# Four sends in a row on GpSimd: the order of low parts and scatter DMAs in a mixture-of-experts loop

## The chip, the cores and the metric

The kernel runs on one core of one Trainium2 chip. The metric is the device time of one execution in microseconds (us). The engines are named as in the profile: PE (TensorE), DVE (VectorE), ACT (ScalarE), POOL (GpSimd) and SP (SyncE, which only starts DMAs here).

## The reference

A block of four layers over x of shape (32, 16, 16, 64), in float32: windowed attention, an involution (per-pixel 3x3 kernels), a channel attention with a first mixture of experts, and a linear attention with a second mixture. Each layer's output is added to its input. The change lies in the last mixture, `_L3_ffn_ref`, of 8192 tokens with 64 channels, 8 experts and a hidden width of 682:

```python
logits = flat @ router_w.T
probs = jax.nn.softmax(logits, axis=-1)
topk_probs, topk_idx = jax.lax.top_k(probs, TOP_K)          # two experts a token
h = jax.nn.silu(h1) * h3                                    # h1, h3: the token through w1, w3
y = jnp.einsum('neh,ech->nec', h, w2)
out = jnp.einsum('ne,nec->nc', gates, y)
```

## The kernel before

The stages follow each other; the experts of the last mixture are one of the last. Before it, POOL has scattered each token's row, as two float16 halves (high and low), to a list in HBM (`slots`), sorted by expert, twice a token (`send5`, L708). The lists are cut into 39 tiles of 512 rows (`NT` = 39), each of one expert; empty tiles and ends hold dump rows. Tile t does this:

- SP loads the tile's 512 rows into one of two buffers XS (`load5`, L549 to 555), once the buffer's last tile is turned and its ids are copied.
- PE turns it (`turn5`, L2151), ACT copies it as XT (L1632).
- The hidden width is cut into six blocks k of 114 (`NHB`, `HB`). For each, PE makes the two up products in four float16 matmuls (L2189), ACT takes the silu of one (L1655), DVE multiplies it by the other into H5 (L1350, counted as `hid5`). ACT rounds H5 to float16, the high part HI5 (`high5`, L1638). The low part LO5 = H5 - HI5 is made by DVE for k = 0, 1, 3, 4 (`low5`, L1360) and by **POOL for k = 2 and 5** (`low5_pool`, L738 to 743). PE's eight down matmuls of the block (`down5`, L2162 to 2172) wait for the low part.
- After block 5, ACT and DVE sum the tile's result into one of two buffers Y5 (L1646 and L1366, counted as `y5`).
- POOL scatters Y5 to `results` in HBM by four indirect DMAs of 128 rows (`results5`, L727 to 733), with row numbers from IDS, which it copies from the loaded tile (`ids5`, L721 to 725).

Every engine takes its instructions in the program's order, and semaphores count what is done. The orders that matter here:

- H5, HI5, LO5 and the up banks are three deep, by k % 3. So DVE's product for block k waits for the low part of block k - 3 (L1349), that for k = 5 for low 2.
- PE runs three blocks behind with the down matmuls (L2184 to 2198): up 3, down 0, up 4, down 1, the next tile's turn, up 5, down 2, and then up 0 of the next tile, down 3, up 1, down 4, up 2, down 5, up 3. Down 5 of a tile thus stands between up 2 and up 3 of the next.
- ACT takes the silu of block n first, then the high part of block n - 1 (L1655 to 1657): the high part of block 5 stands behind the silu of the next tile's block 0. The copy of the sum (L1646) follows at k = 2 of the next tile, and waits until the scatter of two tiles before has landed (`resulted`).
- POOL's loop over t (L745 to 755) has low 2 of tile t, two sends of tile t - 1, low 5 of tile t, the other two sends of tile t - 1, and the copy of the ids of tile t + 1. Pass 0 has no sends, pass 39 sends only.

After the last send, SP waits for all landings (L565), loads the results back in token order, ACT and DVE weigh and add them, and SP stores the output.

Of the kernel before, what the change touches and what calls it, by code (L numbers as in the profile page):

```python
# [113 lines left out]
def network(nc, xw_d, xi_d, mats_d, vecs_d, feats_d, cw1_d, wmask_d, taps_d, wexp_d,  # L114
            w1l2_d, w2l2_d, w1l3_d, w3l3_d, w2l3_d, out_d, slots_d, results_d):
    with ExitStack() as ctx:
# [5 lines left out]
        def S(step):  # L122

            name = PLACE.get(step, (step, 0))[0]
            if name not in sems:
                sems[name] = nc.alloc_semaphore(name)
            return sems[name]

        def when(step, n):

            return S(step), PLACE.get(step, (step, 0))[1] + n
# [445 lines left out]
        def _(pool):  # L577
# [143 lines left out]
            def ids5(t):  # L721
                if t >= 4:
                    pool.wait_ge(*when(f"resulted_{t % 2}", 16 * SUB * (t // 2 - 1)))
                pool.wait_ge(*when(f"loaded_xs_{t % 2}", 16 * (t // 2 + 1)))
                nc.gpsimd.tensor_copy(IDS[t % 4], XS[t % 2].bitcast(U32)[:, :, C]).then_inc(S("ids5"), 1)

            def results5(t, subs):  # L727
                pool.wait_ge(*when("y5", t + 1))
                pool.wait_ge(*when("ids5", t + 1))
                for i in subs:  # L730
                    pool.indirect_dma_start(  # L731
                        results_d, bass.IndirectOffsetOnAxis(ap=IDS[t % 4][:, i:i + 1], axis=0),
                        Y5[t % 2][:, i, :], None).then_inc(S(f"resulted_{t % 2}"), 16)
# [4 lines left out]
            def low5_pool(t, k):  # L738
                n = t * NHB + k
                pool.wait_ge(*when("high5", n + 1))  # L740
                if n >= 3:
                    pool.wait_ge(*when("down5", n - 2))
                nc.gpsimd.tensor_tensor(LO5[k % 3], H5[k % 3], HI5[k % 3], ALU.subtract).then_inc(S("low5_pool"), 1)  # L743

            for t in range(NT + 1):  # L745
                if t < NT:
                    low5_pool(t, 2)
                if t >= 1:
                    results5(t - 1, (0, 1))
                if t < NT:  # L750
                    low5_pool(t, 5)
                if t >= 1:
                    results5(t - 1, (2, 3))
                    if t + 1 < NT:
                        ids5(t + 1)

# [1619 lines left out]
```

## Time and profile before

| | |
|---|---|
| median of 3 runs | 1143.75 us (1141.32 to 1145.54) |
| the profiled execution | 1143.18 us, span 1141.0 us |
| mean granted clock of PE, as a share of 2.4 GHz | 0.913 |
| busy: PE, DVE, ACT, POOL | 932.4, 801.0, 696.8, 684.4 us |
| POOL's lows (L743), sends (L731) | 78 of 1156 ns, 156 of 984 ns |
| the experts' first low 2 (784.26 us) to the last send's end | 331 us |

The span is the time from the first to the last instruction of the profiled execution. Busy times of several engines overlap. A row of the timeline has start, duration, engine, line, operation, output and input, the count, and in brackets the engine's idle time before it with what ended it. Rows of PE show a group of matmuls whose end includes their latency, so one group's row can reach into the next; the distance from start to start is the pace. "issue" in brackets is idle time that no recorded instruction ended.

### The profile page before, as it was taken

The page shows a single profiled execution, that of the slowest core. Times are in us where ns is not written, and L with a number is a line of the kernel's source. Part 1 is how long each engine was busy: PE and PEld are TensorE (multiplying, and loading weights), DVE is VectorE, ACT ScalarE, POOL GpSimd, SP SyncE. Part 2 cuts the span into 40 slices and gives each one's busy share as a digit, 9 for nine tenths or more (in the row PEclk, how much of TensorE's full clock was granted, in tenths as well). Part 3 has the DMA queues.
Part 4 walks back from the last instruction along what each step waited for, and adds up shares of the span by engine and source line. Part 5 has one row for each costly group of instructions (what it writes and reads, how often), then busy time and mean ns, then how long its engine had stood idle before and what let it go on. Part 6 is the DMA issues. An engine that isn't in the chain of part 4 may idle for free.

```text
span 1141.0 us, 21776 instructions
## 1 busy us (share of the span) xinstructions
PE 932.4 (82%) x6816; PEld 564.5 (49%) x6816; DVE 801.0 (70%) x1647; ACT 696.8 (61%) x1295; POOL 684.4 (60%) x784
## 2 busy tenths in 40 slices
PE   5969999969997899589788875007999999999970
PEld 3445555534445754244355453005776776766650
DVE  7976667668856545787668886305888888887865
ACT  1845555546453276556676663006888888888875
POOL 2945555533778520477406777772777777777770
PEclk9979999989999699599899997558999999999995
DMA  5000000020004100000200000100111111111106
GB/s 217 1 2 1 1 1 1 2 70 0 1 25 124 51 1 0 1 1 14 70 1 22 25 26 25 64 26 24 32 37 31 37 31 32 37 31 35 32 24 224
DMA packets 25473, 39.37 MB, mean 35 GB/s; under 512 B 6340, under 2 KB 14296, under 8 KB 25112
## 3 DMA queue, kind: packets, MB, share of 16 engines
q1 hardware_dynamic: 16280, 28.62, 7.9%
q0 software_dynamic: 9088, 9.39, 2.7%
q8 instruction: 61, 1.00, 0.4%
q14 instruction: 44, 0.36, 0.1%
HBM read 24.52 MB, written 13.47 MB: 33 GB/s over the span
## 4 chain that ended last, share of the span: by engine, by line
PE 35%; POOL 31%; issue 14%; DVE 10%; ACT 7%; DMA 1%; POOLq 0%; SPq 0%; DVEq 0%; ACTq 0%
POOL results L731 11%; POOL slots L708 10%; POOL stage L743 7%; PE bank L1737 6%; PE bank L1748 3%; PE bank L1739 2%; PE bank L1814 2%; POOL stage L690 2%; PE bank L1762 2%; DVE T L816 1%; ACT T L328 1%; ACT T L326 1%; PE bank L1831 1%; PE bank L1866 1%; PE bank L1765 1%
## 5 line engine op out<-in xcount | busy, mean ns | idle before, releaser
L2189 PE MATMUL bank<-stage,big 128*114 128x512 f16 x936 | 243.8, 383 | 1.2 <-ACT stage L1632 1.0
L1350 DVE TENSOR_TENSOR T<-bank,T 114x512 f32<-114x512 f32 x234 | 161.6, 690 | 116.9 <-ACT T L1655 115.9
L731 POOL DMA_INDIRECT results<-stage,small x156 | 153.5, 984 | 37.7 <-issue 35.4
L708 POOL DMA_INDIRECT slots<-T,index x128 | 126.7, 990 | 79.2 <-DVE index L1261 41.6
L1655 ACT ACTIVATE T<-bank 114x512 f32<-114x512 f32 x234 | 139.8, 598 | 40.6 <-PE bank L2189 40.5
L2169 PEld LDWEIGHTS bank<-l2w,stage 114*128 114x128 f16 x1872 | 120.8, 97 | 56.3 <-issue 17.7
L1638 ACT ACTIVATE stage<-T 114x512 f16<-114x512 f32 x234 | 145.5, 622 | 0.2 <-DVE T L1350 0.2
L2169 PE MATMUL bank<-l2w,stage 114*128 x1872 | 143.4, 219 | 2.2 <-POOL stage L743 1.2
L2189 PEld LDWEIGHTS bank<-stage,big 128*114 x936 | 108.3, 131 | 46.8 <-issue 9.1
L743 POOL TENSOR_TENSOR stage<-T,stage 114x512 f16<-114x512 f32 x78 | 90.2, 1156 | 49.7 <-ACT stage L1638 49.7
L1360 DVE TENSOR_TENSOR stage<-T,stage 114x512 f16<-114x512 f32 x156 | 106.9, 685 | 0.0
L1413 ACT ACTIVATE stage<-stage 128x512 f32<-128x512 f32 x64 | 40.3, 630 | 79.4 <-DVE stage L841 79.4
L837 DVE TENSOR_REDUCE small<-bank 128x8 f32<-128x512 f32 x64 | 44.3, 692 | 55.9 <-PE bank L1739 55.9
L621 POOL TENSOR_TENSOR stage<-T,vecs 128x128 f32<-128x128 f32 x64 | 26.6, 415 | 85.1 <-PE bank L1739 85.1
L1737 PE MATMUL bank<-stage 128*128 128x512 f32 x128 | 72.9, 652 | 0.0
L625 POOL TENSOR_TENSOR stage<-T,small 128x512 f32<-128x512 f32 x64 | 67.5, 1055 | 0.0
L645 POOL TENSOR_TENSOR stage<-stage 128x512 f16<-128x512 f32 x40 | 46.1, 1159 | 34.2 <-ACT stage L1469 33.2
L2158 PE MATMUL bank<-ident,stage 128*128 128x128 f16 x156 | 15.4, 221 | 60.5 <-DMA stage<-slots 60.5
L1632 ACT ACTIVATE stage<-bank 128x512 f16<-128x512 f32 x39 | 23.0, 589 | 62.4 <-PE bank L2158 62.4
L690 POOL TENSOR_TENSOR stage<-stage 128x256 f16<-128x256 f32 x64 | 43.0, 690 | 26.8 <-DVE stage L1125 26.3
L909 DVE TENSOR_TENSOR stage<-bank,big 128x512 f32<-128x512 f32 x72 | 46.9, 688 | 9.3 <-PE bank L1831 7.0
L1996 PE MATMUL bank<-T,mats 128*128 128x512 f32 x64 | 36.8, 667 | 15.0 <-ACT T L1545 15.0
(381 smaller groups left out, 1989.7 us busy)
## 6 DMA issues: line engine op xcount, KB each, us to landing
stage<-slots SPq DMA_DIRECT2D x39, 130.0 KB, 2.1
stage<-in_w1l SPq DMA_DIRECT2D x8, 342.0 KB
stage<-in_w3l SPq DMA_DIRECT2D x8, 342.0 KB
results<-stage,small POOLq DMA_INDIRECT x156, 2.2
T<-in_xw SPq DMA_DIRECT2D x4, 512.0 KB, 5.7
X<-in_xi SPq DMA_DIRECT2D x1, 2048.0 KB, 14.0
slots<-T,index POOLq DMA_INDIRECT x128, 2.2
X<-results SPq DMA_DIRECT2D x8, 256.0 KB, 5.9
```

The source lines that it names most:

```text
L625: nc.gpsimd.tensor_tensor(KX[s].rearrange("p (h k) -> p h k", h=HEADS), T2[:, bass.ds(n * WT, WT)].unsqueeze(1).broadcast_to([P, HEADS, WT ...
L690: nc.gpsimd.tensor_tensor(HID_LO[n % 4], HID[n % 4], HID_HI[n % 4], ALU.subtract).then_inc(S("low3"), 1)
L708: pool.indirect_dma_start(slots_d, bass.IndirectOffsetOnAxis(ap=index[:, k, n:n + 1], axis=0), rows5[:, n * RW:(n + 1) * RW], None).then_i ...
L731: pool.indirect_dma_start(results_d, bass.IndirectOffsetOnAxis(ap=IDS[t % 4][:, i:i + 1], axis=0), Y5[t % 2][:, i, :], None).then_inc(S(f" ...
L743: nc.gpsimd.tensor_tensor(LO5[k % 3], H5[k % 3], HI5[k % 3], ALU.subtract).then_inc(S("low5_pool"), 1)
L1350: nc.vector.tensor_tensor(H5[q], bank[3 + q][0:HB, :], S5[q], ALU.mult).then_inc(S("hid5"), 1)
L1360: nc.vector.tensor_tensor(LO5[q], H5[q], HI5[q], ALU.subtract).then_inc(S("low5"), 1)
L1638: nc.scalar.activation(HI5[q], H5[q], ACT.Copy).then_inc(S("high5"), 1)
L1655: nc.scalar.activation(S5[q], bank[q][0:HB, :], ACT.Silu).then_inc(S("silu5"), 1)
L1737: nc.tensor.matmul(bank[s][:, :], QB[s], KX[s], start=True, stop=False)
L2169: mm = nc.tensor.matmul(bank[6 + s][:, i * 128:(i + 1) * 128], H[:, i * 128:(i + 1) * 128], downs[:, bass.ds(w, 2 * C)], start=(k == 0 and ...
L2189: mm = nc.tensor.matmul(bank[q + 3 * (v // 2)][0:HB, :], big16[:, bass.ds(e * (4 * HID3) + (v * HID3 + k * HB), HB)], XT[s], start=(v % 2 ...
```

## The change

POOL makes low 2 and low 5 of a tile one after the other, and then sends the four parts of the tile before in a row.

```diff
@@ -745,12 +745,10 @@
             for t in range(NT + 1):
                 if t < NT:
                     low5_pool(t, 2)
-                if t >= 1:
-                    results5(t - 1, (0, 1))
                 if t < NT:
                     low5_pool(t, 5)
                 if t >= 1:
-                    results5(t - 1, (2, 3))
+                    results5(t - 1, (0, 1, 2, 3))
                     if t + 1 < NT:
                         ids5(t + 1)
```

## Rows read from the trace of the kernel before

**Rows 1.** Stretches: length; busy us (count) of PE, PEld, DVE, ACT, POOL; clock; DMA; GB/s.

```profile
245.00:246.00 1.00, 0.10 (x2) 0.10 (x4) 0.69 (x1) 0.13 (x1) 0.20 (x1) 0.84 0.83 235
...
690.00:695.00 5.00, 3.25 (x17) 2.79 (x18) 2.93 (x8) 1.95 (x3) 3.78 (x5) 1.00 0.10 28
...
850.00:1000.00 150.00, 149.78 (x1364) 105.08 (x1361) 121.40 (x198) 132.13 (x251) 115.37 (x126) 1.00 0.12 34
```

**Rows 2.** The page's chain that ended last, by line, shares of the span.

```profile
POOL results L731 11%; POOL slots L708 10%; POOL stage L743 7%; PE bank L1737 6%; PE bank L1748 3%; PE bank L1739 2%; PE bank L1814 2%; POOL stage L690 2%; PE bank L1762 2%; DVE T L816 1%; ACT T L328 1%; ACT T L326 1%; PE bank L1831 1%; PE bank L1866 1%; PE bank L1765 1%
```

**Rows 3.** Waits, 792 to 1108 us: us in total, times, longest us.

```profile
POOL stage L743 <- ACT stage L1638: 39.1, 73, 2.9
```

**Rows 4.** Timeline of POOL alone in the experts stage.

```profile
792.49 1.16 POOL L743 TENSOR_TENSOR stage<-T,stage 114x512 f16<-114x512 f32 x1 [2.85 <-ACT stage L1638]
...
867.90 1.15 POOL L743 TENSOR_TENSOR stage<-T,stage 114x512 f16<-114x512 f32 x1 [0.24 <-ACT stage L1638]
869.22 1.00 POOL L731 DMA_INDIRECT results<-stage,small  x1 [0.16 <-issue]
...
872.26 1.15 POOL L743 TENSOR_TENSOR stage<-T,stage 114x512 f16<-114x512 f32 x1 [0.76 <-ACT stage L1638]
873.57 0.99 POOL L731 DMA_INDIRECT results<-stage,small  x1 [0.16 <-issue]
874.87 0.97 POOL L731 DMA_INDIRECT results<-stage,small  x1 [0.30 <-issue]
875.83 0.21 POOL L725 COPY small<-stage 128x4 uint32<-128x4 uint32 x1
876.27 1.16 POOL L743 TENSOR_TENSOR stage<-T,stage 114x512 f16<-114x512 f32 x1 [0.23 <-ACT stage L1638]
...
1102.98 1.15 POOL L743 TENSOR_TENSOR stage<-T,stage 114x512 f16<-114x512 f32 x1 [0.25 <-ACT stage L1638]
...
1106.59 1.17 POOL L743 TENSOR_TENSOR stage<-T,stage 114x512 f16<-114x512 f32 x1
...
1110.49 0.97 POOL L731 DMA_INDIRECT results<-stage,small  x1 [0.30 <-issue]
1111.77 0.97 POOL L731 DMA_INDIRECT results<-stage,small  x1 [0.31 <-issue]
...
1114.32 0.97 POOL L731 DMA_INDIRECT results<-stage,small  x1 [0.30 <-issue]
```

**Rows 5.** Timeline of the other engines in the same cycle.

```profile
869.19 0.60 PEld L2169 LDWEIGHTS bank<-l2w,stage 114*128 114x128 f16 x8
...
869.26 0.68 DVE L1360 TENSOR_TENSOR stage<-T,stage 114x512 f16<-114x512 f32 x1
...
869.96 1.07 PE L2189 MATMUL bank<-stage,big 128*114 128x512 f16 x4
...
871.06 0.60 ACT L1655 ACTIVATE T<-bank 114x512 f32<-114x512 f32 x1 [0.39 <-PE bank L2189]
...
871.55 0.62 ACT L1638 ACTIVATE stage<-T 114x512 f16<-114x512 f32 x1
...
873.55 0.45 PEld L2169 LDWEIGHTS bank<-l2w,stage 114*128 114x128 f16 x8 [0.36 <-issue]
...
874.01 1.03 PE L2189 MATMUL bank<-stage,big 128*114 128x512 f16 x4
...
875.32 1.03 PE L2189 MATMUL bank<-stage,big 128*114 128x512 f16 x4
...
875.57 0.62 ACT L1638 ACTIVATE stage<-T 114x512 f16<-114x512 f32 x1
```

**Rows 6.** Timeline of PE alone, two idle pieces in earlier stages.

```profile
245.91 1.97 PE L1773 MATMUL bank<-T,mats 128*64 128x512 f32 x4 [2.10 <-DVE T L846]
...
691.24 1.99 PE L2046 MATMUL bank<-T,KVS 128*128 128x256 f32 x8 [1.98 <-DVE KVS L1186]
```

**Rows 7.** DMA issues of the page: KB each, us to landing.

```profile
results<-stage,small POOLq DMA_INDIRECT x156, 2.2
```

## The prediction

> **What bounds the kernel now.** I read the stretches first: in the experts stage PE is busy 149.78 of 150 us at clock 1.00, POOL only 115.37 [rows 1]. The page's chain puts "POOL results L731" at its head with 11% [rows 2]. That could mislead: it walks back through POOL's queue, gaps between sends and all. So I turned to what POOL waits for: L743 waits 39.1 us for ACT over 73 instances [rows 3]. The timeline of one tile then shows who is early. Call the low part of block k "low k". POOL starts low 2 at 867.90, sends two sums, idles 0.76 us until ACT's high part comes, starts low 5 at 872.26, sends two more, copies the ids (0.21 us at 875.83), idles 0.23 us, and starts the next low 2 at 876.27 [rows 4]. Both lows start when ACT delivers; the sends fit in the pauses, with 0.76 and 0.23 us to spare. This cycle is 8.37 us long. From the first low 2 with sends behind it (792.49) to the last (1102.98) there are 37 cycles, 310.49 / 37 = 8.39 us each [rows 4].
>
> PE's own work in a cycle is nearly as long. One k step (four up matmuls, eight down) takes 1.31 us, 874.01 to 875.32; the eight down are 0.46 of it, 873.55 to 874.01, so the four matmuls of the turn, as wide, some 0.2: 6 x 1.31 + 0.2 = 8.1 us [rows 5]. Most of what PE loses is the 0.36 us in front of the down matmuls of k = 5: POOL's low ends at 873.41, their weights load at 873.55 [rows 4, 5]. So **PE bounds the stage, with POOL's low parts right beside it**, and what matters is not how many sends POOL has, but how many stand between two lows.
>
> **What the change does.** It adds and removes no instruction: a pass of POOL's loop stays two lows, four sends, one copy. Two of the sends (two DMA issues a pass) move from between low 2 and low 5 to behind low 5. So the first half of a cycle has no send, and the second has four, in 37 passes.
>
> *Half one, low 2 to low 5.* Low 5 starts when ACT hands over, not when POOL is free, so taking two sends from ahead of it gains nothing [rows 4]. That high part stands on ACT behind the silu of the next tile's first block, this on PE behind the down matmuls that wait for low 2. Once low 2 is late the path is: low and hand-over to PE 1.29 us (as 872.26 to 873.55), down matmuls to the next up 0.46, up to silu 1.10 (869.96 to 871.06), to the high part 0.49 (871.55), to POOL 0.71 (872.26) [rows 4, 5]. Sum 4.05. The 4.36 us of now (867.90 to 872.26) is the upper end. I take 4.09, near the sum, since its terms are those of a PE that has just stalled.
>
> *Half two, low 5 to the next low 2.* Now it is 4.01 us (872.26 to 876.27). With four sends: low 5 and gap 1.31 (872.26 to 873.57), first to second send 1.30 (874.87), then 1.28 twice, as sends follow each other in the tail (1110.49, 1111.77), together 5.17; from the last send to the copy 0.96 (874.87 to 875.83), the copy 0.20: 6.33 us, and a gap before the low [rows 4]. No gap is the lower end, the 0.23 of now the upper; I take 0.10, so 6.43 us. ACT's high part for k = 2 is ready 3.93 us after low 5's start (875.57 + 0.62) and will wait 2.4 us for POOL [rows 4, 5]. Nothing covers that: the down matmuls of k = 2 stand on PE ahead of the next tile's first up, DVE's product for k = 5 waits for the same low (buffer k % 3), and ACT's next high part stands behind the silu of that up.
>
> The cycle becomes 4.09 + 6.43 = **10.52 us** against 8.39; 37 x 2.13 = **+78.8 us**. By the ends, 10.38 to 10.92, it is +73.6 to +93.6.
>
> *The tail.* Now the last send starts at 1114.32, 7.73 us after the last low 5 (1106.59), the sixth behind it. It will be the eighth: 1.31 + 1.30 + 6 x 1.28 = 10.29, **+2.6 us**. The last low 2 to low 5 takes 3.61 us now (1102.98 to 1106.59), waiting for a silu that will be done by then; low, product, high part and gaps (1.15, 0.68 as DVE's other pass over this shape, 0.62, some 0.3) make 2.8, **-0.8 us** [rows 4, 5].
>
> *Priced at nothing.* The sums that are sent are ready a cycle before the same buffer is written again: the last send starts 9.3 us after a pass's low 2 and lands 2.2 us later, and ACT's next write of that buffer stands behind the low 5 of the next pass, at 14.6 us or later; if that cover went, ACT would wait for a landing [rows 4, 7]. The copy of the ids keeps its place behind the fourth send, so SP's queue, whose next load waits for it, moves with the cycle, and its load has most of a cycle.
>
> *The shared port.* A send of 1.00 us (869.22) ran through a whole L1360 of DVE (869.26, 0.68 us), against 0.97 for one at 874.87: the overlap costs 0.03 us at most, and I add nothing [rows 4, 5]. The Trainium skill, "SBUF — State Buffer", section "Who interferes with whom", has it that a VectorE instruction with two SBUF inputs and a GpSimd instruction that reads SBUF shut each other out for a whole instruction. By it each send that meets an L1360 would take up to 0.68 us more: two in a tile are 1.4 us, or +50 us. The row speaks against it for sends.
>
> *The clock.* PE will idle 10.5 - 8.1 = 2.4 us a tile, nearly all in one piece ahead of the down matmuls of k = 2. An idle piece of 1.98 us left the clock at 1.00 (2.4 GHz) at 691.24; one of 2.10 us before 245.91 lost it (0.84 within 245 to 246, so a fall to 0.50, 1.2 GHz) [rows 1, 6]. The new stall is no shorter than these, but with denser work around it. At half speed the k step on the path of half one doubles, at most +1.3 us in a tile; elsewhere the stall absorbs it. Between 0 and 1.3 us a tile I take 0.22, as if one tile in three were hit, for half of its step: 37 x 0.22 = **+8 us**, range 0 to +24.
>
> **Sum.** 78.8 + 2.6 - 0.8 + 8 = +88.6 us. The profiled execution took 1143.18 us (span 1141.0, and 2.2 around it): 1231.8. The median of the runs is 0.57 above it: **1232.4 us**. Low end: 1143.75 + 73.6 + 1.8 = 1219. High end: 1143.75 + 93.6 + 1.8 + 24 = 1263.
>
> **Rivals.**
> - *The clock falls in every tile.* Half one grows by the whole 1.3 us each time: 80.6 + 48 = +129, 1272 us. For it: the 2.10 us that lost the clock. Against it: the 1.98 us that kept it, and a stall between stretches in which PE never rests [rows 1, 6]. Chance 0.10. The Trainium skill, "TensorE: Matmul & The Clock Gate", section "A second HAM failure mode: psum-queue depth-cycling", tells of just this: frequent short idles let the clock swing, and throughput falls; this stage, with idles of 0.36 us, doesn't show it so far.
> - *The late low 2 is hidden*, no change, 1144 us. It takes 2.4 us of room between the end of low 2 and PE's need of it. PE loads weights for it at 869.19, 0.14 us after the low's end at 869.05 [rows 4, 5]. Chance 0.03.
> - *Faster.* If the sends held back low 5, moving them would give PE its 0.36 us ahead of k = 5 back: 38 x 0.36 = 14, 1130 us. What decides is POOL's idle time ahead of low 5: at zero the sends are to blame; it is 0.76, ended by ACT [rows 4]. Low 2 would have to be without effect as well. Chance 0.02.
> - The new order could be without effect if POOL didn't keep its program's order; its rows do. This is within the 0.03.
>
> **Chances.** The forecast's case 0.85, the clock in every tile 0.10, hidden 0.03, faster 0.02. About 0.5%, 5.7 us, is what can be told from no change; the first two cases are far above it, so slower 0.95, same 0.03, faster 0.02. The range 1219 to 1263 leaves out the clock rival, the two small ones and the forecast's own edges, under 0.2.
>
> **What would show it.** L743 still 78 times at 1.16 us, by turns 4.1 and 6.4 us apart, with no idle time ahead of low 2; sends in fours, 1.28 to 1.30 us apart; the down matmuls (L2169) waiting some 2.2 us a tile for POOL's L743; PE busy for about 77% of the stage, POOL as long as before; granted clock a little under 1.00. I would be wrong if the cycle at full clock lay outside 10.4 to 10.9 us, if the stall stood at another block, if something waited for a send's landing or a load, or if the stage's clock were under 0.9.

## The result, and the profile after

The changed kernel takes **1217.89 us** (median of 4 runs, 1213.3 to 1219.65), beside 1142.53 us for the kernel before (4 runs, 1139.32 to 1145.54): ratio **1.0664**, 95% interval 1.0633 to 1.0695. It is slower, as forecast, but by 75.4 us rather than 88.6, and the time lies 1.1 us below the range's low end. The profiled execution of the changed kernel took 1219.65 us, with a span of 1217.8 us.

Its page, lines of busy time and of the groups that matter (busy us, mean ns of one | idle before them and what ended most of it):

```profile
PE 944.6 (78%) x6816; PEld 569.6 (47%) x6816; DVE 806.0 (66%) x1647; ACT 695.6 (57%) x1295; POOL 682.3 (56%) x784
...
L2167 PE MATMUL bank<-l2w,stage 114*128 x1872 | 148.4, 224 | 68.8 <-POOL stage L743 68.5
...
L743 POOL TENSOR_TENSOR stage<-T,stage 114x512 f16<-114x512 f32 x78 | 90.2, 1157 | 125.7 <-ACT stage L1636 125.7
...
L1358 DVE TENSOR_TENSOR stage<-T,stage 114x512 f16<-114x512 f32 x156 | 114.5, 734 | 0.0
```

POOL does the same work in the same busy time (682.3 us; it was 684.4). What is new is PE's idle time in front of the down matmuls, 68.5 us of it ended by POOL's low part. (The change takes two lines out, so L2169 of before is L2167 here, L1638 is L1636, and so on.)

The same stage as in [rows 1, 3]. First two stretches, with the columns of [rows 1]; then the waits from 792 to 1180 us (us in total, times, longest):

```profile
850.00:1000.00 150.00, 120.87 (x1104) 83.30 (x1102) 98.72 (x161) 107.64 (x205) 93.35 (x104) 1.00 0.09 27
834.00:836.00 2.00, 2.00 (x11) 1.10 (x9) 0.92 (x2) 0.00 (x0) 0.00 (x0) 0.50 0.26 67
```

```profile
POOL stage L743 <- ACT stage L1636: 110.1, 37, 3.9
...
PE bank L2167 <- POOL stage L743: 67.8, 37, 3.2
DVE T L1348 <- POOL stage L743: 45.8, 30, 2.7
```

PE, busy all of the 150 us before, is busy 120.87 of them. It waits once in each of 37 tiles, 1.83 us on the mean, and DVE's product waits for the same low. L743 waited for ACT 73 times before, now 37 times: the other half of the lows, all low 2s, show no wait, since ACT's part is ready before POOL is. A stretch at clock 0.50 (1.2 GHz) shows that the clock does fall at times.

POOL alone, one cycle, to hold against [rows 4]:

```profile
864.31 1.16 POOL L743 TENSOR_TENSOR stage<-T,stage 114x512 f16<-114x512 f32 x1
868.33 1.16 POOL L743 TENSOR_TENSOR stage<-T,stage 114x512 f16<-114x512 f32 x1 [2.86 <-ACT stage L1636]
869.63 1.00 POOL L731 DMA_INDIRECT results<-stage,small  x1
870.94 0.96 POOL L731 DMA_INDIRECT results<-stage,small  x1 [0.30 <-issue]
872.21 0.96 POOL L731 DMA_INDIRECT results<-stage,small  x1 [0.30 <-issue]
873.47 0.96 POOL L731 DMA_INDIRECT results<-stage,small  x1 [0.31 <-issue]
874.43 0.20 POOL L725 COPY small<-stage 128x4 uint32<-128x4 uint32 x1
874.58 1.16 POOL L743 TENSOR_TENSOR stage<-T,stage 114x512 f16<-114x512 f32 x1
```

Low 2 (864.31), low 5 (868.33), four sends, copy, next low 2 (874.58). Half one is 4.02 us, half two 6.25 here and 6.28 in most tiles; the usual cycle is **10.30 us** against 8.39. The other engines in half one, as in [rows 5]:

```profile
865.60 0.45 PEld L2167 LDWEIGHTS bank<-l2w,stage 114*128 114x128 f16 x8 [2.41 <-issue]
865.61 0.62 PE L2167 MATMUL bank<-l2w,stage 114*128 x8 [1.95 <-POOL stage L743]
...
866.06 1.03 PE L2187 MATMUL bank<-stage,big 128*114 128x512 f16 x4
...
867.13 0.60 ACT L1653 ACTIVATE T<-bank 114x512 f32<-114x512 f32 x1 [2.33 <-PE bank L2187]
...
867.63 0.62 ACT L1636 ACTIVATE stage<-T 114x512 f16<-114x512 f32 x1
```

The path stands there link by link: low 2 to the down matmuls 1.29 us, to the up behind them 0.46, to the silu 1.07, to the high part 0.50, to low 5 0.70. Together 4.02. PE's stall of 1.95 us is in front of the down matmuls of k = 2.

The two ends of the row of cycles, and the tail, POOL alone:

```profile
789.75 1.16 POOL L743 TENSOR_TENSOR stage<-T,stage 114x512 f16<-114x512 f32 x1 [2.85 <-ACT stage L1636]
...
1178.21 1.16 POOL L743 TENSOR_TENSOR stage<-T,stage 114x512 f16<-114x512 f32 x1
1180.93 1.15 POOL L743 TENSOR_TENSOR stage<-T,stage 114x512 f16<-114x512 f32 x1 [1.56 <-ACT stage L1636]
...
1191.18 0.97 POOL L731 DMA_INDIRECT results<-stage,small  x1 [0.30 <-issue]
```

37 cycles take 388.46 us (310.49 before): +78.0. The last low 5 to the last send is 10.25 us (7.73): +2.5. The last low 2 to low 5 is 2.72 (3.61): -0.9. The stage's first low 2 with sends came 2.7 us earlier than before, by the spread of the stages ahead of it, which the change doesn't touch. The sum, +76.9, is the difference of the spans (1217.8 - 1141.0 = 76.8).

### The profile page after: what moved, and what is told of

The parts are those of the page before. It is cut to its first block, busy times and chain, and to the rows that moved or that the text cites. A ratio compares the mean times of both kernels' runs of the same rounds, so it can differ in the third digit from the quotient of the medians.

```text
span 1217.8 us, 21737 instructions
## 1 busy us (share of the span) xinstructions
PE 944.6 (78%) x6816; PEld 569.6 (47%) x6816; DVE 806.0 (66%) x1647; ACT 695.6 (57%) x1295; POOL 682.3 (56%) x784
## 4 chain that ended last, share of the span: by engine, by line
PE 46%; POOL 20%; DVE 15%; issue 10%; ACT 7%; DMA 1%; SPq 0%; POOLq 0%; DVEq 0%; ACTq 0%
POOL results L731 10%; PE bank L2187 7%; PE bank L1735 5%; PE bank L2167 5%; POOL stage L743 5%; POOL slots L708 4%; PE bank L1746 2%; PE bank L1737 2%; PE bank L1812 2%; PE bank L1760 2%; PE bank L1975 1%; PE bank L1950 1%; ACT T L328 1%; DVE T L814 1%; ACT T L326 1%
## 5 line engine op out<-in xcount | busy, mean ns | idle before, releaser
L2187 PE MATMUL bank<-stage,big 128*114 128x512 f16 x936 | 251.3, 392 | 1.0 <-ACT stage L1630 1.0
L2167 PE MATMUL bank<-l2w,stage 114*128 x1872 | 148.4, 224 | 68.8 <-POOL stage L743 68.5
L2167 PEld LDWEIGHTS bank<-l2w,stage 114*128 114x128 f16 x1872 | 122.8, 100 | 132.6 <-issue 101.4
L743 POOL TENSOR_TENSOR stage<-T,stage 114x512 f16<-114x512 f32 x78 | 90.2, 1157 | 125.7 <-ACT stage L1636 125.7
L1636 ACT ACTIVATE stage<-T 114x512 f16<-114x512 f32 x234 | 145.5, 622 | 1.7 <-DVE T L1348 1.7
L2187 PEld LDWEIGHTS bank<-stage,big 128*114 x936 | 111.3, 135 | 44.1 <-issue 7.9
L1358 DVE TENSOR_TENSOR stage<-T,stage 114x512 f16<-114x512 f32 x156 | 114.5, 734 | 0.0
```

The lines of the kernel that those rows point to most:

```text
L1358: nc.vector.tensor_tensor(LO5[q], H5[q], HI5[q], ALU.subtract).then_inc(S("low5"), 1)
L1636: nc.scalar.activation(HI5[q], H5[q], ACT.Copy).then_inc(S("high5"), 1)
L2167: mm = nc.tensor.matmul(bank[6 + s][:, i * 128:(i + 1) * 128], H[:, i * 128:(i + 1) * 128], downs[:, bass.ds(w, 2 * C)], start=(k == 0 and ...
L2187: mm = nc.tensor.matmul(bank[q + 3 * (v // 2)][0:HB, :], big16[:, bass.ds(e * (4 * HID3) + (v * HID3 + k * HB), HB)], XT[s], start=(v % 2 ...
```

## The experiments

The account to be tested: low 2 is late by the sends that stand between low 5 and it; the rest of the loop is drawn out by that, and by nothing else in the row of sends. The rivals: that low 5's place doesn't matter, only low 2's; that four indirect DMAs in a row cost something as such (a queue, landings); that the idle time lowers the clock and this is much of the price. "Before" is the kernel before on the same chip, in the same sitting. Halves and cycles are medians over the 37 tiles unless called means, each from start to start of POOL's lows. A fall of the clock is counted where stretches of 1 us show under 1.00. Nothing of the computation is left out in any of these kernels; where work was added, nothing reads what it writes.

**e1: all four sends between low 2 and low 5.** Against the changed kernel:

```diff
                     low5_pool(t, 2)
+                if t >= 1:
+                    results5(t - 1, (0, 1, 2, 3))
                 if t < NT:
                     low5_pool(t, 5)
                 if t >= 1:
-                    results5(t - 1, (0, 1, 2, 3))
                     if t + 1 < NT:
```

> All four sends stand between low 2 and low 5, none behind low 5. Theory A (what counts is POOL's queue between two lows; each half of a cycle is the longer of that queue and the other engines' chain): low 2 to low 5 becomes 1.31 + 3 x 1.27 + 0.97 and a gap, 6.1 to 6.25 us, the stall moves to the down matmuls of k = 5, low 5 to low 2 stays at 4.0; cycle 10.1 to 10.3 us, +65 to +78 us against the kernel before. Rival B (only low 2 is urgent, since the next tile's first up stands behind it on PE; a late low 5 is harmless): +0 to +10 us.

Measured: 1208.94 us, before 1140.7, ratio 1.0606 (1.0549 to 1.0663). POOL alone, one cycle, and the largest wait of PE for it:

```profile
881.08 1.16 POOL L743 TENSOR_TENSOR stage<-T,stage 114x512 f16<-114x512 f32 x1 [2.25 <-ACT stage L1637]
...
886.23 0.95 POOL L731 DMA_INDIRECT results<-stage,small  x1 [0.30 <-issue]
887.20 1.17 POOL L743 TENSOR_TENSOR stage<-T,stage 114x512 f16<-114x512 f32 x1
...
891.23 1.16 POOL L743 TENSOR_TENSOR stage<-T,stage 114x512 f16<-114x512 f32 x1 [2.25 <-ACT stage L1637]
```

```profile
PE bank L2168 <- POOL stage L743: 63.5, 37, 2.9
```

The halves have changed places: 6.14 and 4.02 us, the same sum within 0.15 (the copy of the ids is no longer in the long half). Now low 5 is the one without idle time before it, and the stall stands at its down matmuls. Low 5 is as urgent as low 2; the rival by which only low 2 matters falls.

**e2 and e3: one and three sends.** The edit of e2; e3 has `(0, 1, 2)` in the first place and `(3,)` in the second:

```diff
                     low5_pool(t, 2)
+                if t >= 1:
+                    results5(t - 1, (0,))
                 if t < NT:
                     low5_pool(t, 5)
                 if t >= 1:
-                    results5(t - 1, (0, 1, 2, 3))
+                    results5(t - 1, (1, 2, 3))
```

> One send between low 2 and low 5, three behind low 5. Theory A: low 5 to low 2 is 6.28 - 1.27 = 5.01 us, low 2 to low 5 4.02, cycle 9.03 us, +23 to +27 us, with an idle piece on PE of 1.0 us and no fall of the clock in the experts stage. Rival C (a row of sends costs as such, by landing or by descriptors, growing with its length more than in proportion): the third send in a row longer than 1.27 us from its forerunner, and more or less than +23 us by that.

> Three sends between low 2 and low 5, one behind low 5. Theory A: low 2 to low 5 is 1.31 + 2 x 1.27 + 0.97 and a gap, 4.85 to 5.0 us against 4.36, low 5 to low 2 4.0; cycle 8.9 to 9.0, +19 to +25 us. Rival B (low 5 isn't urgent): +0 to +3 us.

Measured: e2 1166.86 us, ratio 1.0237 (1.0175 to 1.0298); e3 1163.07 us, ratio 1.0203 (1.0123 to 1.0283); before 1140.7. The halves are 4.04 and 5.00 us in e2, 4.88 and 4.03 in e3. With the halves of e1 and of the changed kernel this is a price list: behind low 5, three sends give 5.00 us and four 6.28; behind low 2, three give 4.88 and four 6.14. A send past the room costs 1.26 to 1.28 us, the distance between two sends, and the other half is 4.02 to 4.04 whatever the split. In the cycle the third send costs less, 0.67 us in e2 (9.04 against 8.37) and 0.54 in e3 (8.91), since part of it fills the pause that was there; only the fourth costs its whole length. Two in each half just fit. By their intervals both are slower than before, by 26.2 and 22.4 us, and both are close to 2%.

**e4: the order of before, with other POOL work in place of sends.** Two subtractions of constants, 1.16 us each, stand behind the second pair of sends:

```diff
+            def filler(m):
+                ...
+                    nc.gpsimd.tensor_tensor(fills[j % 3], mats[0:HB, 10:14, :].rearrange("p m n -> p (m n)"),
+                                            mats[0:HB, 14:18, :].rearrange("p m n -> p (m n)"),
+                                            ALU.subtract).then_inc(S("dest5_later"), 1)
                 if t >= 1:
                     results5(t - 1, (2, 3))
+                    filler(2)
```

> The sends stay as in the kernel before (two and two); behind the second pair POOL makes two subtractions of two constant arrays of 114x512, as long as a low part (1.16 us), into memory that nothing reads. Theory A: low 5 to low 2 becomes 3.74 + 2 x 1.2 = 6.1 to 6.3 us without any third send in a row, PE stalls ahead of the down matmuls of k = 2, cycle 10.1 to 10.35, +65 to +80 us. Rival C (the row of four sends or its transfers are what costs): under +10 us.

Measured: 1224.73 us, before 1140.7, ratio 1.0744 (1.0651 to 1.0838). POOL alone, half two:

```profile
897.16 1.16 POOL L743 TENSOR_TENSOR stage<-T,stage 114x512 f16<-114x512 f32 x1 [0.17 <-ACT stage L1653]
...
899.77 0.96 POOL L731 DMA_INDIRECT results<-stage,small  x1 [0.30 <-issue]
900.75 2.50 POOL L755 TENSOR_TENSOR KSS<-mats 114x512 f16<-114x512 f32 x2
903.20 0.18 POOL L725 COPY small<-stage 128x4 uint32<-128x4 uint32 x1
903.35 1.14 POOL L743 TENSOR_TENSOR stage<-T,stage 114x512 f16<-114x512 f32 x1
```

Halves 4.01 and 6.18 us, with no sends moved at all. 2.50 us of arithmetic does what two sends (2.54 us) do. So a long half needs no row of four DMAs: what counts is POOL's time ahead of low 2. The 84.0 us are more than the 65 to 80 expected, though the cycle came as expected (10.31 on the mean); the two runs lie 7 us apart, and the interval goes from 74 to 96 us. One tile took 7.78 us in *half one*: in the half two before it one low of DVE had lasted 3.54 us against 0.68, held while POOL's subtractions, copy and low ran, and the clock fell there as well. DVE:

```profile
846.80 3.54 DVE L1375 TENSOR_TENSOR stage<-T,stage 114x512 f16<-114x512 f32 x1
```

**e7: a row of four sends, no second low on POOL.** DVE makes low 2; in the changed kernel:

```diff
-        POOL_LOW = (2, 5)
+        POOL_LOW = (5,)
...
-                if t < NT:
-                    low5_pool(t, 2)
```

> The four sends stay in a row behind low 5, as in the changed kernel, but DVE makes low 2; POOL has one low, four sends and a copy a tile. Theory A: POOL's queue from low 5 to the next low 5 is 6.28 us, less than the cycle of 8.37, so nothing waits: cycle 8.1 to 8.5 us, -10 to +5 us against the kernel before, DVE 0.69 us a tile busier. Rival C (the row of sends costs as such): +50 us or more remain. Rival D (DVE becomes the bound): cycle over 8.6 us.

Measured: 1143.13 us, before 1141.52, ratio **1.0007** (0.9988 to 1.0026), cycle 8.37 us. The same row of four sends and the same copy behind low 5 cost nothing when POOL has 2.03 us of idle time left before its next low. This is the other half of e4's verdict.

**e8: the other low to DVE.** `POOL_LOW = (2,)`, the call `low5_pool(t, 5)` taken out, and on DVE the last block's low behind the loop:

```diff
-        POOL_LOW = (2, 5)
+        POOL_LOW = (2,)
...
-                if t < NT:
-                    low5_pool(t, 5)
...
+            low5(NT * NHB - 1, (NHB - 1) % 3)
```

> DVE makes low 5, POOL only low 2 and then the four sends in a row. Theory A, and that PE's 0.36 us a tile in the kernel before stands for POOL's slower low 5 (1.16 us against 0.69 on DVE): that wait goes, nothing else appears, cycle 8.05 to 8.25 us, -5 to -12 us against the kernel before. Rival D (DVE, at 7.5 of 8.1 us, delays a product or a low): cycle 8.4 us or more, 0 to +10 us.

**e11: DVE makes all six lows** (`POOL_LOW = ()`, both calls taken out, the same line on DVE).

> DVE makes all six lows, POOL only sends and copies. Theory A and D (by its rows DVE then has 8.2 us of work a tile, beside 8.1 us of PE's): DVE becomes the bound, cycle 8.3 to 8.7 us, 0 to +12 us against the kernel before. Rival: the cycle is 8.2 us or less, since POOL's low 2 was still in PE's way; -6 us or better.

Measured: e8 **1135.89 us**, before 1141.52, ratio 0.9954 (0.9936 to 0.9973); e11 1139.04 us, before 1142.73, ratio 0.9966 (0.9947 to 0.9986). Both beat the kernel before by a little, 5.6 and 3.7 us. From 850 to 1000 us, e8 and then e11, columns of [rows 1]:

```profile
850.00:1000.00 150.00, 149.78 (x1373) 107.42 (x1371) 133.23 (x217) 132.06 (x255) 97.08 (x109) 1.00 0.12 34
```

```profile
850.00:1000.00 150.00, 149.81 (x1372) 107.61 (x1372) 142.48 (x235) 132.09 (x254) 75.64 (x92) 1.00 0.12 34
```

The cycle goes from 8.37 to 8.29 in e8 and 8.30 in e11, 0.08 us a tile or 3 us in 37; the interval of e8, 3 to 7 us, just holds that, and the rest is within the spread. In both PE waits for POOL's lows no more, and DVE has room for one low (133.23 of 150 us) and still for two (142.48, or 7.9 us a tile rather than the 8.2 expected). Two expectations missed: in e11 DVE did not become the bound, and e8's cycle was to be 8.05 to 8.25.

The miss of e8 goes back to how the prediction read PE's rows. It took the 0.36 us of idle time of the weight load ahead of k = 5 [rows 5] for what PE loses. The matmuls lose less, since those of the block before still run meanwhile. In the kernel before, PE:

```profile
872.62 1.03 PE L2189 MATMUL bank<-stage,big 128*114 128x512 f16 x4
```

The next ups start at 874.01 and 875.32 [rows 5]. The step across the idle time is 1.39 us from start to start, the one behind it 1.31: 0.08 us, and this is what e8 gains. The 8.1 us of PE's own work were right, but 0.20 us more stand around the next tile's first up in every tile: in e8 the ups start at 874.89, 876.35 and 877.70, steps of 1.46 and 1.35 us. Its weights load 0.32 us after ACT's copy of the turned tile has ended (876.02 to 876.34), which this up reads; that PE waits for this copy there is likely but wasn't tried. 8.1 + 0.2 is the 8.29 of e8.

**e5 and e6: the stall made longer.** The changed kernel with one and with two fillers of e4 behind its row of sends (`filler(1)`, `filler(2)` ahead of `ids5`).

> The changed kernel with one idle-making subtraction (1.16 us) more behind the four sends of a pass. Without the clock: low 5 to low 2 7.5 us, cycle 11.5 us, +115 to +122 us against the kernel before. Theory E (the longer the idle piece on PE, here 3.1 us, the more tiles in which the clock falls, each 1.0 us dearer): stage clock at most 0.92, more than 12 tiles with a half cycle 0.8 us or more over its usual length, +130 to +165 us. Rival F (the six falls of the changed kernel have nothing to do with the stall's length): about six falls again, stage clock 0.95 or more, +120 to +128 us.

> The changed kernel with two such subtractions more. Without the clock: cycle 12.7 us, +160 to +168 us. Theory E: the clock falls in nearly every tile (idle piece 4.3 us), stage clock under 0.85, low 2 to low 5 at 5.0 us or more in most tiles, +195 to +215 us. Rival F: about six falls, +165 to +172 us.

Measured: e5 1277.01 us, ratio 1.1184 (1.1131 to 1.1238); e6 1338.83 us, ratio 1.1726 (1.1684 to 1.1768); before 1141.52. Half two is 7.49 and 8.71 us, so each filler takes 1.21 to 1.22. The clock is the other part: 0.92 on the mean of 850 to 1000 us in e5, and in e6:

```profile
850.00:1000.00 150.00, 106.42 (x834) 73.23 (x832) 104.52 (x122) 80.58 (x154) 96.33 (x99) 0.88 0.07 21
```

A tile of e6 in which the clock fell, PE, ACT and POOL:

```profile
887.77 1.14 POOL L743 TENSOR_TENSOR stage<-T,stage 114x512 f16<-114x512 f32 x1
...
889.05 1.03 PE L2182 MATMUL bank<-l2w,stage 114*128 x8 [4.23 <-POOL stage L743]
...
889.88 1.91 PE L2202 MATMUL bank<-stage,big 128*114 128x512 f16 x4
...
891.83 0.60 ACT L1668 ACTIVATE T<-bank 114x512 f32<-114x512 f32 x1 [5.86 <-PE bank L2202]
...
893.02 1.15 POOL L743 TENSOR_TENSOR stage<-T,stage 114x512 f16<-114x512 f32 x1 [4.11 <-ACT stage L1651]
```

The up matmuls take 1.91 us where they took 1.03, the silu comes late, and half one is 5.25 instead of 4.01. In e6 this happens in 25 of 37 tiles: 25 x 1.24 / 37 = 0.84, and 4.01 + 8.71 + 0.84 = 13.56, beside a mean cycle of 13.61. So a fall on this path costs **1.24 us**, close to the 1.3 that the prediction gave for one, and its case of a fall in every tile is approached but not reached, with two tiles in three at the longest stall tried. The times, +135.5 and +197.3 us, are within those of theory E; the clock of e6, 0.88, stayed above the 0.85 expected.

**e9 and e10: the clock's price in the changed kernel.** e10 is the changed kernel once more. e9 adds six matmuls that nothing reads, in the stall:

```diff
                     if k == NHB - 1 and not final:
+                        pe.wait_ge(*when("hid5", n - 1))
+                        for i in range(6):
+                            nc.tensor.matmul(bank[0][:, :], ident16[:, 0:128], XT[s], start=True, stop=True)
```

> The changed kernel, and ahead of the down matmuls of k = 2 PE makes six more matmuls of 128x512 (1.3 us) into an up bank that is free then, with a result that nothing reads; they fit in the 1.9 us for which PE waits there. Theory E (the idle piece on PE is what lets the clock fall, and a fall costs about 0.8 us a time): clock 1.00 all through the experts stage, no half cycle 0.8 us over its usual length but the one near tile 29 that all kernels have, half cycles 6.28 and 4.02 as before, 4 to 7 us faster than the changed kernel run beside it. Rival F (the falls come from something else): as many falls, the same time. Rival G (the six matmuls stand in the way): a cycle of more than 10.4 us and a slower kernel.

> The changed kernel unaltered, as the neighbour of the last one. Theory A: half cycles 6.28 and 4.02 again, 1213 to 1220 us. Theory E: four to nine falls of the clock in the experts stage, at other places than in its first profile.

Measured: e9 1221.23 us, ratio 1.0675 (1.0649 to 1.07); e10 1221.21 us, ratio 1.0685 (1.0661 to 1.071); before 1142.73. Stretches of e9, then of e10:

```profile
850.00:1000.00 150.00, 140.25 (x1192) 92.05 (x1190) 97.65 (x160) 106.31 (x202) 91.82 (x103) 1.00 0.10 27
```

```profile
1000.00:1150.00 150.00, 123.13 (x1075) 84.78 (x1072) 96.99 (x156) 105.58 (x201) 91.76 (x102) 0.97 0.10 27
```

Kept busy, PE never loses its clock in the 37 cycles, and the halves are still 4.02 and 6.28: the lateness of low 2 is the price, and the clock at most a few us of it. The gain of 4 to 7 us expected from e9 did not come; in the first cycle, where there is no stall of 1.9 us yet, its six matmuls made half one 5.46 us long. e10, at 1221.21 us, is a little over the 1213 to 1220 expected. It lost the clock in 4 tiles only, and the mean cycles are 10.384 (e9) and 10.412 (e10), 1 us over 37; the medians can't tell that apart. How often the clock falls differs from one execution to the next.

PE's wait for POOL a tile (total by times, 37 or 36) and the falls, over all kernels: 0.48 us (e3) and 0.74 (e2), none; 1.72 (e1), none; 1.84 (e4), 2 falls; 1.83 and 1.87 (changed, e10), 7 and 4; 2.74 (e5), 18, two of them twice as long; 3.88 (e6), 25, eleven of them twice as long; 0.68 (e9), none. One execution of each kernel stands behind these counts.

## Why the prediction was right and where it was off

**The mechanism held.** Slower by the lateness of low 2; L743 78 times at 1.16 us with turns of 4.02 and 6.28 us; sends in fours, 1.26 to 1.31 apart; the stall at the down matmuls of k = 2; POOL's busy time as before; nothing waited for a landing or a load. e1, e4 and e7 show the cause from three sides.

**Half one**, predicted 4.09 (lower end 4.05), is 4.02. Each link came within 0.03 us, and I had added 0.04 to their sum.

**Half two is the step that failed**: predicted 6.43, with 6.33 as a lower end; it is 6.28, and 6.25 in the tile shown. I had written "the copy 0.20: 6.33 us, and a gap before the low" and called no gap the lower end. In the rows the low starts 0.15 us after the *start* of the copy (874.43 to 874.58): the two overlap, and the end of the copy was never a bound. In [rows 4] the same low waited for ACT, so its distance to the copy said nothing on what POOL needs. This is the whole 0.15: 0.05 from the end of the copy and 0.10 of a gap that isn't there. The sends came as I had them within 0.02 us. With half one this makes the usual cycle 10.30, outside my ends of 10.38 to 10.92: 37 x 0.22 = 8 us too much, and at the low end 37 x 0.08 = 3 us, 1.9 of them from half two and 1.1 from half one.

**The miss of the range is in part chance.** Without these 3 us the low end would have been 1216, and the result inside. But it is outside by 1.1 us only; one of the four runs, 1219.65, is inside, and the kernel before took 1142.53 us beside the changed one, 1.2 less than the 1143.75 that I added to. The difference of 75.4 us is just what my low end had, 73.6 + 1.8, and it is so because two errors cancel: that end had a cycle too long and no fall of the clock.

**The clock.** I took +8 us for falls. In the profiled execution everything above the usual cycle is 388.46 - 37 x 10.30 = 7.4 us. Seven falls make some 5.6 of it: three come out as a late silu (half one 5.04, 5.00 and 4.94 us), two as two sends each that take 1.46 or 1.47 us instead of 0.97, since in these two tiles DVE's lows, late themselves, start just ahead of them (half two 7.28 and 7.27 us; below), the last two as a few tenths. An irregular gap in POOL makes 1.2 (below). In e10 the same kernel had 10.412 - 10.30 = 0.11 us a tile, 4 us, for both. A fall cost 0.8 us on the mean, where I had half of 1.3; the falls came in 7 and 4 of 37 tiles instead of one in three. A fall of that kind, in the profile of the changed kernel:

```profile
833.67 0.81 PE L2167 MATMUL bank<-l2w,stage 114*128 x8 [1.92 <-POOL stage L743]
834.28 1.91 PE L2187 MATMUL bank<-stage,big 128*114 128x512 f16 x4
...
836.23 0.60 ACT L1653 ACTIVATE T<-bank 114x512 f32<-114x512 f32 x1 [3.33 <-PE bank L2187]
...
837.42 1.16 POOL L743 TENSOR_TENSOR stage<-T,stage 114x512 f16<-114x512 f32 x1 [3.89 <-ACT stage L1636]
```

**The tail and the last half**: +2.5 for a predicted +2.6, -0.9 for -0.8.

**The rest**: the stage began 2.7 us earlier in this execution, the median of the changed kernel lies 1.8 under its profiled one, and the spread of single runs is some 3 us each way. I had put nothing of this into the range. From forecast to result: 8.1 (half one and two) + 0.7 (clock and gap) + 0.2 (tail, last half) + 2.7 + 1.8 + 0.6 (the median of before over its profiled execution) + 0.35 (what lies around the span) = 14.4 of 14.5 us.

**Stall and share**: I expected 2.2 us of waiting a tile and 77% for PE. It is 1.83 us and 81% (120.87 / 150), because the cycle is 0.22 us shorter than forecast and PE spends 0.2 us a tile around the first up (e8), not in the stall. The 0.36 us ahead of k = 5 that I called most of PE's loss were 0.08 us of its matmuls.

**The shared port** cost the sum little, some 2 us within the 5.6, but my reading of it holds only for a send that starts first; see below.

**The rivals.** Hidden and faster did not occur. The clock in every tile did not occur here, and in e6 it came in 25 of 37.

## What to carry to other kernels

When an in-order engine both computes for others and issues DMAs, count what stands between two results that others wait for, not the engine's busy share: POOL was 77% busy in the stage and yet a fourth send in either half cost its whole 1.27 us (a third, 0.54 to 0.67). A lower bound for a new path must be read where that path binds: a gap or an order seen while the engine waited for something else isn't a floor. Nor is the idle time of a weight load what the matmuls lose: take their pace from start to start. Moving one of the two urgent results to an engine with room (e8) took away both the hazard and the last small stall.

## What the runs showed of the hardware

**Who is held when DVE and POOL overlap.** The prediction used a send that had started first (869.22, DVE's low at 869.26) [rows 4, 5] and concluded that the two don't disturb each other. For that order it holds: in the kernel before 148 lows of DVE start while a send runs, and all take 0.68 or 0.69 us. Where DVE's low starts just ahead of the send, the send is held. In the changed kernel, DVE and POOL:

```profile
817.35 0.68 DVE L1358 TENSOR_TENSOR stage<-T,stage 114x512 f16<-114x512 f32 x1
817.40 1.47 POOL L731 DMA_INDIRECT results<-stage,small  x1 [0.30 <-issue]
```

With POOL's own low it is DVE that is held. In e2, in nearly every tile, DVE's low starts second, and a send is held behind it as well:

```profile
906.00 1.17 POOL L743 TENSOR_TENSOR stage<-T,stage 114x512 f16<-114x512 f32 x1
906.37 1.35 DVE L1360 TENSOR_TENSOR stage<-T,stage 114x512 f16<-114x512 f32 x1
...
907.33 1.27 POOL L731 DMA_INDIRECT results<-stage,small  x1 [0.17 <-issue]
```

In e1, in 36 tiles, DVE's low starts *first*, 0.42 us ahead of POOL's (887.20, above), and is held all the same:

```profile
886.78 2.15 DVE L1359 TENSOR_TENSOR stage<-T,stage 114x512 f16<-114x512 f32 x1
```

Both times DVE's low ends 0.55 or 0.56 us after POOL's (907.72 after 907.17; 888.93 after 888.37), while POOL's takes its 1.15 to 1.18 us. The same holds in the changed kernel, where one DVE low took 2.04 us (821.73, POOL's low at 822.06); seven such lows took their mean from 685 to 734 ns. So the order of the starts in the rows doesn't tell who waits: POOL's low is never lengthened, DVE's is whenever the two overlap. The Trainium skill, "SBUF — State Buffer", section "Who interferes with whom", has it that a VectorE instruction with two SBUF inputs and a GpSimd instruction that reads SBUF exclude each other, and that the order of issue decides who waits. That they exclude each other agrees with the held send and with both orders of the lows; that the first one wins agrees with e2 but, going by the recorded starts, not with e1, and a send that starts first holds nobody. Why is open. The prediction's +50 us by that rule did not come, since most sends that meet a low of DVE start before it.

**A small copy and the next operation overlap on POOL**: 0.15 us from start to start (874.43, 874.58), with a copy of 0.20.

**Falls of the clock beside short idle pieces.** No wait of PE for POOL behind the falls in the changed kernel was above 3.2 us, and most were near 1.9. At a mean wait of 1.72 us a tile (e1) there were no falls, at 3.88 (e6) there were 25 in 37 tiles. That PE's idleness is what lets the clock fall is borne out by e9: no fall, against 7 and 4 in the two executions of the same kernel without the added matmuls. The Trainium skill, "TensorE: Matmul & The Clock Gate", section "A second HAM failure mode: psum-queue depth-cycling", speaks of such short idles; the trace agrees, with falls to 0.50, 4 to 7 of them here. Why a given tile is hit and its neighbour isn't stays open.

**A gap in POOL's sends.** Once in the stage, a send starts 2.55 us behind the one before it instead of 1.27, and the profile of the changed kernel names only "issue" for it:

```profile
1088.07 1.00 POOL L731 DMA_INDIRECT results<-stage,small  x1 [0.15 <-issue]
1090.62 0.97 POOL L731 DMA_INDIRECT results<-stage,small  x1 [1.55 <-issue]
```

It is the same send, the 114th, in the kernel before as well, where it moves the low by 0.5 us, and in all the other kernels but e4, which doesn't show it, and e11, where it is 0.3 us. Where the sends lie on the path it costs 1.2 (e1, half one 7.35 us) to 2.1 us (e2, half two 7.07). Its cause wasn't tried.
